# A gated convolution and a mixture-of-experts FFN on one core: z stored once in quarter rows, its tiles transposed by VectorE, the gates computed inside the FFN

## The reference, cut to what matters

```python
# stage 1: gated long convolution over the columns, head by head
kv  = einsum('bhil,bhjl->bijhl', ctx_, ctx_)           # products of the 8 rows of a head
y   = irfft(rfft(kv, 2L) * rfft(ssm_kernel, 2L))[..., :L] + kv * D
x   = x + tanh(g_xattn) * einsum('bijhl,bhil->bjhl', y, layernorm(x)_)
# stage 2: FFN on z = layernorm(x), T = 8192 tokens, F = 512
shared = ffn(z, shared_w1, shared_w2)                  # (x1 * silu(x2)) @ w2, [x1|x2] = z @ w1
aff = sigmoid(z @ gate_w + expert_bias)                # 7 routed experts
mask = top 2 experts of each token
sel  = for each expert, the top T//7 = 1170 tokens by score
routed = sum over experts of ffn(z[sel], w1[e], w2[e]) * aff, scattered to the tokens
out = x + tanh(g_ffn) * (shared + routed)
```

## Time and profile before

| | before |
|---|---|
| median of 3 runs | 4091.8 us (4090.35 to 4098.31) |
| the profiled execution | 4100.51 us, span 4098.7 us |
| TensorE busy | 4040.9 us (99%) |
| TensorE weight loads | 3679.4 us (90%, beside the matmuls) |
| VectorE busy | 2575.6 us (63%) |
| ScalarE busy | 1953.6 us (48%) |
| GpSimd busy | 1455.2 us (36%) |
| granted TensorE clock, mean | 0.997 |
| stage 1 | up to about 1921 us |
| shared groups 0 to 15 | about 1922 to 2962 us |
| routed groups | the rest |

### The profile page before, as it was taken

How to read it: one execution, slowest core, us unless ns; L and a number is a source line. 1 busy time by engine, 2 the same in 40 slices (tenths; PEclk the granted TensorE clock), 3 DMA queues, 4 the chain that set the end, 5 groups by cost and what they waited for, 6 DMA issues and landing times.

```text
span 4098.7 us, 71212 instructions
## 1 busy us (share of the span) xinstructions
PE 4040.9 (99%) x25370; PEld 3679.4 (90%) x25370; DVE 2575.6 (63%) x3032; ACT 1953.6 (48%) x2601; POOL 1455.2 (36%) x1465
## 2 busy tenths in 40 slices
PE   8999999999999999999999999999999999999999
PEld 7999999999999999998788777888888988988887
DVE  8999999999999999998443432222334433434342
ACT  7888888888888888885111111111122121212120
POOL 2444444444444444441000024443214434334341
PEclk9999999999999999999999999999999999999999
DMA  7888888888888888886223233433444545545443
GB/s 190 224 217 222 216 223 219 220 216 223 220 219 220 219 221 218 221 213 200 85 85 101 86 100 100 107 90 98 117 120 109 105 94 115 100 99 115 79 99 49
DMA packets 267383, 632.27 MB, mean 154 GB/s; under 512 B 32890, under 2 KB 99162, under 8 KB 267256
## 3 DMA queue, kind: packets, MB, share of 16 engines
q1 hardware_dynamic: 206376, 414.05, 32.8%
q0 software_dynamic: 60880, 216.44, 29.4%
HBM read 311.44 MB, written 170.16 MB: 117 GB/s over the span
## 4 chain that ended last, share of the span: by engine, by line
PE 48%; DVE 1%; DMA 1%; issue 1%; POOL 1%; ACT 0%; SPq 0%; POOLq 0%; DVEq 0%; PEldq 0%; ACTq 0%
PE mem_acc L2031 11%; PE mem_acc L2032 11%; PE mem_acc L2033 11%; PE moe_ps L2050 3%; PE moe_ps L2051 3%; PE moe_ps L2052 3%; PE moe_psT L2052 2%; PE moe_psT L2051 2%; PE moe_psT L2050 2%; POOL moe_zin L1591 0%; DMA out<-moe_y 0%; DVE moe_zl L1917 0%; DMA moe_ranks<-z_d,moe_get_i 0%; DMA moe_y<-out 0%; DMA moe_zin<-z_d,moe_get_i 0%
## 5 line engine op out<-in xcount | busy, mean ns | idle before, releaser
L2031 PE MATMUL mem_acc<-moe_zh,moe_w1h 128*128 128x512 f32 (+2 forms) x2336 | 849.5, 364 | 16.2 <-issue 6.9
L2032 PE MATMUL mem_acc<-moe_zl,moe_w1h 128*128 128x512 f32 (+2 forms) x2336 | 845.8, 362 | 0.0
L2033 PE MATMUL mem_acc<-moe_zh,moe_w1l 128*128 128x512 f32 (+2 forms) x2336 | 845.5, 362 | 0.0
L909 PE MATMUL mem_acc<-att_kv_hi,att_tz_hi 128*128 128x288 f32 x2560 | 768.5, 300 | 19.9 <-DVE att_pick L848 18.0
L911 PE MATMUL mem_acc<-att_kv_hi,att_tz_lo 128*128 128x288 f32 x2560 | 757.0, 296 | 0.0
L910 PE MATMUL mem_acc<-att_kv_lo,att_tz_hi 128*128 128x288 f32 x2560 | 756.9, 296 | 0.0
L1940 DVE TENSOR_TENSOR moe_hid<-mem_acc,moe_act_s 128x512 f32<-128x512 f32 (+2 forms) x148 | 91.5, 618 | 758.5 <-PE mem_acc L2033 610.5
L909 PEld LDWEIGHTS mem_acc<-att_kv_hi,att_tz_hi 128*128 128x128 f32 x2560 | 482.5, 188 | 32.0 <-DVE att_pick L848 18.0
L2031 PEld LDWEIGHTS mem_acc<-moe_zh,moe_w1h 128*128 128x128 f32 x2336 | 442.5, 189 | 75.9 <-issue 19.3
L2033 PEld LDWEIGHTS mem_acc<-moe_zh,moe_w1l 128*128 128x128 f32 x2336 | 442.3, 189 | 56.9
L2032 PEld LDWEIGHTS mem_acc<-moe_zl,moe_w1h 128*128 128x128 f32 x2336 | 442.7, 190 | 56.0 <-issue 0.2
(11 more groups left out here) (235 smaller groups left out, 8668.7 us busy)
## 6 DMA issues: line engine op xcount, KB each, us to landing
att_kv_lo<-att_kv POOLq DMA_DIRECT2D x126, 1152.0 KB, 9.7
att_kT<-in_cT SPq DMA_DIRECT2D x64, 512.0 KB, 6.5
att_xn<-in_x SPq DMA_DIRECT2D x64, 512.0 KB, 8.3
out<-att_x SPq DMA_DIRECT2D x64, 512.0 KB, 7.2
z_d<-att_z SPq DMA_DIRECT2D x64, 512.0 KB, 5.9
zT_d<-att_zT SPq DMA_DIRECT2D x64, 512.0 KB, 8.5
moe_y<-out SPq DMA_DIRECT2D x128, 256.0 KB, 4.3
out<-moe_y SPq DMA_DIRECT2D x128, 256.0 KB, 5.1
```

The costliest lines, as they stand in the source:

```text
L909: nc.tensor.matmul(acc, w_hi[:, cols], x_hi, start=start, stop=False, skip_group_check=True)
L2031: nc.tensor.matmul(acc, w1h[j][:, c, b, :], zh[:, c, 0:w], start=(c == 0), stop=False)
L2032: nc.tensor.matmul(acc, w1h[j][:, c, b, :], zl[:, c, 0:w], start=False, stop=False)
L2033: last = nc.tensor.matmul(acc, w1l[j][:, c, b, :], zh[:, c, 0:w], start=False, stop=(c == C - 1))
```

## The change

- Stage 1 no longer has `turn_z`, `columns`, `store_zT`, `gates`, `gate_parts`, `sum_gates` and `logits`. z is stored once, by four DMAs with pieces of 1 KB (`z_rows[q]`), so that a whole "row" of `z_d` in a tile holds quarter q of the columns of four tokens. A tile loaded with 4 KB rows and transposed by VectorE in 32x32 blocks then has columns on the partitions.
- The weights' rows are loaded in the matching order, by 8 DMAs instead of 2 for each j (`load_ffn_w1`).
- Every z tile of the shared groups is transposed in place by VectorE before it is split: `ffn_z_turn` for group 0's, in the last step of stage 1, and `turn_shared` for the others. Tiles 0 and 1 of the next group are turned before `gate_up(cur, 3)`, tiles 2 and 3 in the window, after halves 2 and 3.
- The gates are computed in groups 1 to 5, for two heads at a time: 32 pairs in `gate_slots` (4 in group 1, 7 in each of groups 2 to 5), behind a first product. GpSimd loads a pair (two DMAs of 512 KB) into one of two buffers, as soon as the gates of the pair two before are done; VectorE transposes it (128x2048); TensorE does 8 matmuls of 256 columns (`gates`) and, one slot later, two that sum (`sum_gates`).
- Group 0 does only `make_setup`; `make_scores` stands at the start of group 6 and the 42 routing steps in groups 6 to 10, three for each j. The first product with b = 0 is cut in halves for the second of them. LEAD is 11.
- The list writes are 128 indirect DMAs without staging copies and waits between them. VectorE computes the quarter rows' numbers (`codes`) at the start of group 15, and the 16 DMAs that spread them (`merged_at` to `spread`) come after that.

```diff
-    z_rows = z_d[0:B * S, :].rearrange("(b h j) l -> h b j l", b=B, j=HD)
+    QD = L // 4
+    z_rows = [bass.AP(z_d.tensor, q * (P // 4 * L), [[P * L, H], [QD, 4], [L, P // 4], [1, QD]]) for q in range(4)]
+    z_tiles = bass.AP(z_d.tensor, 0, [[P * L, H], [L, P], [1, L]])
...
             def store_z(h):
                 sp.wait_ge(z_set, h + 1)
-                sp.dma_start(z_rows[h], z[:, :]).then_inc(z_out, 16)
-
-            def store_zT(h):
-                sp.wait_ge(zT_set, 2 * h + 2)
-                sp.dma_start(zT_d[h], zT[:, :, :]).then_inc(zT_out, 16)
+                for q in range(4):
+                    sp.dma_start(z_rows[q][h], z[:, q * QD:(q + 1) * QD]).then_inc(z_out, 16)
...
+            def ffn_z_turn(t):
+
+                dve.wait_ge(ffn_z_in[t], 16)
+                nc.vector.transpose(mem.first_z[t], mem.first_z[t]).then_inc(ffn_z_turned, 1)
...
                 if ahead:
                     pairs(h + 1, 1)
                 else:
+                    ffn_z_turn(0)
+                    ffn_z_turn(1)
                     ffn_z_low(0)
                     ffn_z_low(1)
                     ffn_w1_low(0, 1)
                 if back:
                     residual(h - 1, 1 - u, 1)
                 if not ahead:
+                    ffn_z_turn(2)
+                    ffn_z_turn(3)
                     ffn_z_low(2)
                 multiply(h, u, 0)
...
                 conv(h, u, 0)
                 conv(h, u, 1)
                 if back:
                     turn_o(h - 1, 0)
-                if back2:
-                    turn_z(h - 2, 0)
                 conv(h, u, 2)
                 conv(h, u, 3)
                 shared(h, u, 0)
-                if back2:
-                    turn_z(h - 2, 1)
                 conv(h, u, 4)
-                if back2:
-                    gates(h - 2)
                 turn_x(h, 0)
...
-        EACH = 2 * (FC - 1)
-        PLACES = [["scores"]] + [STEPS[a:a + EACH] for a in range(0, len(STEPS), EACH)] + [[]]
+        EACH = 3 * (FC - 1)
+        GATED = 5
+        PLACES = [["setup"]] + [[] for _ in range(GATED)] + [STEPS[a:a + EACH] for a in range(0, len(STEPS), EACH)]
         LEAD = len(PLACES)
-        assert LEAD == 9 and GS >= LEAD + 3 and (GS - 1 - LEAD) % 2 == 0
+
+        def gate_slots(k):
+
+            if not isinstance(k, int) or not 1 <= k <= GATED:
+                return {}
+            places = [(j, b) for j in range(FC) for b in (1, 0)]
+            places = places[4:] if k == 1 else places[:7]
+            start = 0 if k == 1 else 4 + 7 * (k - 2)
+            return {place: start + n for n, place in enumerate(places)}
...
+            def load_pair_of_tiles(n, half):
+
+                wait(pool, parts_done, n - 1)
+                for i in range(2):
+                    pool.dma_start(halves_of_raw[half][:, i * D:(i + 1) * D], z_tiles[2 * n + i]).then_inc(pair_in[half], 16)
...
+            for h in range(H):
                 for n in range(2):
...
+                    nc.gpsimd.indirect_dma_start(list_of[n], bass.IndirectOffsetOnAxis(slot_of[:, h, n:n + 1], 0),
+                                                 pay[:, h, n, :], None).then_inc(scattered[n], 16)
...
+            def gates(n):
+
+                pe.wait_ge(pair_turned, n + 1)
+                if n == 0:
+                    pe.wait_ge(gates_in, 16 * QUARTERS)
+                wait(pe, parts_set, n)
+                for c in range(C):
+                    q = c % 4
+                    z = halves_of_raw[n % 2].rearrange("p (g c n) -> p c g n", c=C, n=SQ)[:, c]
+                    last = nc.tensor.matmul(psT[q * GQ:(q + 1) * GQ, 0, 0:2 * P], gate_q[:, c, :], z,
+                                            start=(c < 4), stop=(c >= C - 4))
+                last.then_inc(parts_done, 1)
+
+            def sum_gates(n):
+
+                pe.wait_ge(parts_set, n + 1)
+                wait(pe, logits_set, n)
+                for i in range(2):
+                    last = nc.tensor.matmul(psS[:, i, 0:E], part_s[:, i * P:(i + 1) * P], pick[:, :], start=True, stop=True)
+                last.then_inc(sums_done, 1)
...
                         if prev is None and j < 2:
                             pe.sem_inc(up_gate if b == 1 else up, 1)
+                        elif places and j > 0 and b == 0 and prev is not None:
+                            first_product(cur, j, b, 0, C // 2)
+                            if left:
+                                sum_partitions(left.pop(0))
+                            first_product(cur, j, b, C // 2, C)
                         else:
                             first_product(cur, j, b)
...
+                        if (j, b) in gating:
+                            if gating[j, b] > 0:
+                                sum_gates(gating[j, b] - 1)
+                            gates(gating[j, b])
```

More of the change, by code:

```diff
@@ L1196, in experts @@
         passed = m.sem("passed")
-        logit_in = m.sem("logit_in")
+        gates_clear, gates_in = m.sem("gates_clear"), m.sem("gates_in")
+        pair_in = [m.sem(f"pair_in{n}") for n in range(2)]
+        pair_turned = m.sem("pair_turned")
+        parts_done, parts_set, sums_done, logits_set = (
+            m.sem(n) for n in ("parts_done", "parts_set", "sums_done", "logits_set"))
+        coded, code_made = m.sem("coded"), m.sem("code_made")
         numbered = m.sem("numbered")
@@ L1376, in window @@
                 order += halves[a:a + 1]
-                if nxt and nxt.kind == "routed":
-                    order += [("turn", t, None) for t in late if t >= EARLY[nxt.i]]
+                order += [("turn", t, None) for t in late if t >= early_tiles(nxt)]
             return order
@@ L1774, in make_scores @@
                 link(v.tensor_tensor(under[:, :], under[:, :], same[:, :], ALU.mult))
+                assert done[0] == SETUP_STEPS
+            def make_scores():
+                dve.wait_ge(parts_done, BATCHES)
                 dve.wait_ge(negexp, 1)
@@ L1848, in route @@
                     find_bit(step)
-                elif step == "scores":
-                    make_scores()
+                elif step == "setup":
+                    make_setup()
                 elif step == "compare":
@@ L1976, in group @@
                 turning = turnover(cur, nxt)
-                quartered = nxt is not None and nxt.kind == "routed"
+                gating = gate_slots(cur.k) if cur.kind == "shared" else {}
+                if cur.kind == "shared" and isinstance(cur.k, int) and cur.k == GATED + 1:
+                    make_scores()
+                if cur.kind == "shared" and isinstance(cur.k, int) and cur.k == GS - 1:
+                    codes()
+                turn_ahead(gating, 0)
                 for j in range(FC if prev is not None else FC - 1):
-                    if j == FC - 1 and quartered:
+                    if j == FC - 1 and nxt is not None:
                         turn(nxt, 0)
@@ L1989, in group @@
                     if prev is not None:
[L1990 removed]
+                        for step in places[3 * j:3 * j + 3]:
                             route(step)
@@ L1997, in group @@
                     weights_listed()
-                if quartered and EARLY[nxt.i] == 3:
-                    turn(nxt, 2)
+                if BATCHES - 1 in gating.values():
+                    logits(BATCHES - 2)
+                    logits(BATCHES - 1)
+                if nxt is not None:
+                    for t in range(nxt.nt) if prev is None else range(2, early_tiles(nxt)):
+                        turn(nxt, t)
                 for what, t, half in window(prev, nxt):
@@ L2025, in _, with first_product @@
         def _(pe):
-            def first_product(grp, j, b):
+            def first_product(grp, j, b, first=0, behind=C):
                 w = columns_of(grp)
                 acc = ps1[j % 2][:, b, 0:w]
-                for c in range(C):
+                for c in range(first, behind):
                     nc.tensor.matmul(acc, w1h[j][:, c, b, :], zh[:, c, 0:w], start=(c == 0), stop=False)
@@ L2086, in group @@
                 pe.wait_ge(zl_set, cur.tile + cur.nt)
-                left = list(places)
+                left = list(places) if prev is not None else []
+                gating = gate_slots(cur.k) if cur.kind == "shared" else {}
                 for j in range(FC):
```

314 lines of the change are left out of this document (149 added, 165 removed).

## The result

The changed kernel takes **4101.4 us** (median of 20 runs, 4091.6 to 4107.5), the kernel before 4091.6 us (20 runs, 4089.4 to 4098.3). The ratio is 1.0022, 95% interval 1.0015 to 1.0028: slower by some 10 us, where 28 us less were forecast. On one further chip it was slower by 4.1%, and on another four edits of it were slower by 2.5 to 4.0%; that comes with the experiments.

The account below looks back on a forecast made before the run. TensorE was taken to bound both stages, with VectorE the bound by a hair in changed stage 1. Terms -95 + 5 + 48 + 3 + 12 + 2 + 6 - 9 = -28 us gave a median of 4064 us, range 4032 to 4101.

Parts of the forecast that it names:

- what a step of stage 1 is spared: Stage 1: TensorE is spared 1.68 us a step, the step falls by 1.55 us over 61 steps: -95 us.
- the windows: Shared groups' windows: later tile turns stall half 6 by 1.2 us in ten windows, +12 us; half 2's wait, +2 us.
- the routed stage: From group 16's first product on: no change forecast, 0 us.
- the stalls: Windows that list writes met: earlier stalls of some 7 us fall into looser windows, -9 us with the slower clock.
- three signs: Forecast wrong if stage 1's step stays above 28 us, gates wait for their pairs, or a gates slot costs 2 us or more.
- Which engine bounds: Stage 1's step: VectorE at 27.64 us bounds by a hair over TensorE at 27.58; 27.7 us taken.
- Last step and hand-over: End of stage 1 to stage 2's first matmul: VectorE's added turns and w1's eight DMAs cost +5 us, bounds 0 and +10.
- Gates: Groups 1 to 5: 32 slots at 1.5 us, +48 us, plus +3 us for waits on pair loads.
- Late pairs: Rival at `gates(n)`: pair loads land late and the change is slower, 4104 us at 12.5 us landing; chance 0.12.
- the routing: Groups 6 to 10: find-bits covered; `make_scores` and two scans cost +6 us, bounds 0 to 12.
- TensorE alone: Rival: TensorE alone sets stage 1's step at 27.58 us and the windows hide their turns, 4030 us; chance 0.20.
- The windows cost twice as much: Rival: windows cost double, as residual loads come late too, 4078 us; chance 0.09.

Follow-up runs that it names:

- one-store run: Changed kernel with z stored by one DMA of 4 KB pieces instead of four of 1 KB: 4091.5 us, ratio 1.0004 to the kernel before.
- e4: Changed kernel with the last step of stage 1 reordered: ScalarE's high parts behind the first queries, VectorE's `multiply(h, 0)` ahead of turns and low parts: 4259.5 us.
- e1: Changed kernel without the gates: no pair loads, pair turns, gate matmuls or sums, logits copied from a z tile: 4198.0 us.
- e3: Changed kernel with VectorE turning tile 3 right behind tile 2, ahead of tile 2's split, in shared groups' windows: 4252.4 us.
- e5: Changed kernel with VectorE relieved in stage 1: both statistics instructions shortened to 64 columns: 4099.8 us.
- e2: Changed kernel with groups 6 to 10 turning the next group's tiles 0 and 1 ahead of the find-bits of products 1 and 2: 4248.2 us.
- e8: The one-store run's kernel with a token's four quarters addressed side by side instead of 128 KB apart: 4253.6 us.
- e9: Changed kernel with e2's and e3's edits, each list write waiting for the same list's write two heads back to land: 4235.5 us.

## Why the forecast was wrong, step by step

Four terms of the sum failed: what a step of stage 1 is spared (1.55 us forecast, 1.37 measured: 12.9 us of the miss on the spans), the windows (12 + 2 - 9 us forecast, 16.3 measured: find-bits and turns in one queue, which I had put at nothing, and a larger stall at half 6), the routed stage (0 forecast, 5.8 measured), and the stalls, whose gain was subtracted twice (5 us on the median). None of the three signs by which I meant to know that I was wrong came up: the step is under 28 us, no gates wait for their pair, and a slot costs less than 2 us. The one on the step left room for 10 us of miss in stage 1, and the windows, the stalls and the routed stage had none.

**What TensorE is spared in stage 1 (failed by its size).** I took 1.68 us a step. From the distances between the starts of TensorE's rows in 20 steps, the three z lines took 0.71 + 0.58 + 0.14 = 1.43 us. The 0.25 between is what I had added for the wide first matmul behind each (0.21 for 0.13 us) and for the 0.09 ahead of the gates. Such matmuls stayed: 7.0 a step before, 7.75 after (counted from 0.15 us between two starts), and what they take beyond 0.13 us each went from 0.63 to 0.76 us a step. The rows name ScalarE as what part of the weight loads now wait for; that the z work had covered this before is my reading:

```profile
PEld mem_acc L871 <- ACT att_y L534: 12.5, 70, 0.2
PEld mem_acc L871 <- ACT mem_acc L542: 12.1, 53, 0.3
```

Before, only the first of these two was there, at 9.5 us. In all the step fell by 1.37 us, some 60 times: 82.1 us.

**Which engine bounds (failed, cheap).** I named VectorE "by a hair" at 27.64 against TensorE's 27.58, and took 27.7. It is TensorE at 27.88. Naming TensorE from the same rows would have given 27.58, 0.3 us too short in place of 0.2. What failed is TensorE's own sum, by the matmuls above.

**Last step and hand-over: right in sum (+7.4, bounds 0 and +10), not by its parts.** VectorE's `multiply(h, 0)` starts at 1809.35; before it was 1883.19, less the 82.1 of the stage 1801.1, so 8.2 us later. But I had counted only w1's last part, whose eight loads take 4.49 us to issue where two took 1.68, about the 3 us that I gave it. The first part takes 7 us longer (8.96 for 1.90), which I hadn't counted, and by the one-store run 4.9 us of the step are the four stores. So the right sum is partly luck. The order of ScalarE's queue, to which I also gave a share, is not a place to win it back, as e4 shows. TensorE's rows:

```profile
1800.80 1.09 PE L929 MATMUL att_psQ<-att_ident,att_xhat 128*128 128x128 f32 x4 [4.83 <-ACT att_qx L559]
...
1847.80 0.77 PE L2061 MATMUL mem_acc<-moe_zh,moe_w1h 128*128 128x512 f32 x1 [4.89 <-DVE moe_hid L1959]
```

**Gates: right.** Sixteen narrow matmuls in one row of 1.07 us (I took 1.0), no row of them waits for its pair, and a slot is 1.60 us with its share of all else (1.5). "Late pairs" is out. With the wait of 2.4 us the gates took 53.6 us by e1, against my 48 + 3, which leaves some 3.7 us for the routing, against my 6: that the sum of the first products is off by only 0.3 us is two misses that cancel.

```profile
2001.55 0.51 PE L2085 MATMUL moe_psT<-mem_pick,moe_pay 128*128 128x7 f32 x4
2001.99 1.07 PE L2076 MATMUL moe_psT<-moe_raw,moe_quads 128*32 128x256 f32 x16
```

**Windows: half 6 right in its chain and short in size, half 2 missed.** Half 6 waits 0.7 to 1.0 us in each, and a window with this wait alone is 1.7 us over 21.76 (I took 1.2), from just the chain that I added up from the earlier trace rows; e3 takes 1.3 of it away. The 0.56 us of half 2, which I had put into five more windows at +2, show in none without find-bits, not even in the five that had them before.

```profile
2026.46 0.50 PE L2102 MATMUL moe_ps<-moe_w2h,moe_hh 128*128 128x512 f32 x1 [1.01 <-DVE moe_y L1973]
```

What I missed is in three windows. I wrote that tiles 0 and 1 are turned "in VectorE's idle time; cost none", and that the find-bits fit. Each holds by itself, or nearly; together they stand in one queue:

```profile
2318.67 0.17 DVE L1778 SCALAR_TENSOR_TENSOR moe_keep<-moe_psT,moe_cand 128x7 f32<-128x7 f32 x1 [0.80 <-PE moe_psT L2109]
...
2319.28 2.37 DVE L1934 STREAM_TRANSPOSE moe_zin<-moe_zin 128x1024 f32<-128x1024 f32 x2
...
2323.87 2.36 DVE L1886 TENSOR_TENSOR moe_zl<-moe_zin,moe_zh 128x1024 fp32r<-128x1024 f32 x2 [0.26 <-ACT moe_zh L1628]
2326.15 1.40 DVE L1973 SCALAR_TENSOR_TENSOR moe_y<-moe_ps,moe_tg,moe_y 128x512 f32<-128x512 f32 x2
2326.95 0.50 PE L2102 MATMUL moe_ps<-moe_w2h,moe_hh 128*128 128x512 f32 x1 [2.82 <-DVE moe_y L1973]
...
2328.82 0.63 PE L2102 MATMUL moe_ps<-moe_w2h,moe_hh 128*128 128x512 f32 x1
```

The last find-bit waits for the tally that follows the last first product; the turns stand behind it, the splits behind the turns, result 0 behind the splits, and TensorE waits 2.82 us. Soon behind the wait eight matmuls take 0.6 us in place of 0.39, at a granted clock of 0.50, the lower level of 1.2 GHz:

```profile
2328.00:2331.30 3.30, 3.30 (x9) 2.61 (x8) 0.00 (x0) 0.00 (x0) 0.00 (x0) 0.50 0.92 297
```

That is 4.3 to 5.3 us more than in the other windows, three times. By e5's 26.33 us, 2.9 of them are the wait alone, and the rest is the clock behind it. e2 took back 3.7 each.

**The stalls that should have gone (-9, counted twice).** They did go. But the 10.4 us of them that the first profile shows are 4.2 in the second; and they were most of what set that profile 8.7 us over the median, which I also subtracted at the end. The changed kernel's profiled execution, 4105.1 us, is only 3.7 us over its median. So 5 us of the miss on the median (37.4; 32.7 on the spans) is this. It rests on two profiles of the kernel before.

**The routed stage (0) is not explained.** It is 5.8 us longer. TensorE's idle time, at the start of experts, grew by 3.0 us (6.9 to 9.8); the other 2.9 us are in two stretches whose mean granted clock is 0.99 in place of 1.00. The longest wait:

```profile
3283.63 0.73 PE L2061 MATMUL mem_acc<-moe_zh,moe_w1h 128*128 128x512 f32 x1 [3.18 <-DVE moe_zl L1950]
```

Before, this row has 1.50 us. Ten profiles of the new form on free chips give 1127.3 to 1133.4 us, mean 1130.8, two of the kernel before 1126.4 and 1127.1: some 4 us more on average, and the lowest of the ten is just above the higher of the two. So it is likely an effect of the change and not of the one execution. The cause stays open: that the gathers' quarters lie 128 KB apart now was tried (e8) only on a chip where it couldn't be told.

**The rivals.** None of the five came as written. *TensorE alone* named the right engine, at a step of 27.58 us that was too short. *The windows cost twice as much* had the right stage and, for another reason, nearly the size. That the list writes, now issued 1.27 us apart, could starve the residual loads was in none of them: the writes' own pace had only been read as a gain ("130 to 170 us in place of 400").

## What to carry to other kernels

A step that fits in an engine's idle time is free only if nothing ahead of it in that engine's queue waits for a late event: list what stands in the queue between the last such wait and the next result, and add it up once for every kind of group. Name a sign of being wrong for each term that was put at nothing, too. When work is taken out of a stream, count its rows from start to start and nothing for the slow instruction behind it, unless the stream closes without a break. Before a stall is credited as a gain and a profile is scaled to the median, look whether the stall is what set the profile off the median; a second profile of the unchanged kernel shows it.

## What the runs showed of the hardware

On two of five chips, with small indirect writes issued by GpSimd 1.27 us apart (128 of them, 128 pairs of int32 each), SyncE's 256 KB transfers let through only about one result in 34 us (2654.49, 2688.28, 2722.08), with the DMA engines busy 0.16 of the time. In that window two pairs of stores on SyncE's queue took 31.45 and 20.28 us to issue, single ones 0.6. In the first profile of the changed kernel the same transfers landed in 4.4 to 4.6 us beside the same writes. At most four of the writes were under way in e9, and the window was as long. The kernel before, whose writes are 3.14 us apart on average (2.44 in the middle), took 4091 to 4094 us on all five. It makes its lists in another form too, and none of the new form with slower writes ran on the two chips; that the pace is the cause is not shown. What makes the difference between the chips, or the times at which they were used, is open.
